# One block fewer in the expert pipeline of a transformer layer: 135 instead of 136

## The chip, the cores and the metric

The kernel runs on one core of a Trainium2 chip. The metric is the device time of one execution in microseconds (us). A core has five engines that run their own instruction streams and meet at semaphores: TensorE (PE, with its weight loads PEld), VectorE (DVE), ScalarE (ACT), GpSimd (POOL) and SyncE (SP), and 16 DMA engines that move data for the queues of SP, POOL and ACT.

## What is computed

The input is `x` of 4 batches x 2048 tokens x 256 values, all float32. One adaLN transformer layer is applied: attention with one head of 128, then a feed-forward part with one shared and eight routed experts, of which each token takes two. The second half, cut to its core:

```python
h = _layernorm(x) * (1 + cb) + sb
shared = (silu(h @ shared_gate.T) * (h @ shared_up.T)) @ shared_down.T
probs = sigmoid(h @ router_w.T + routing_bias)
scores, indices = top_k(probs, 2);  scores /= scores.sum(-1)
g, u = silu(h @ gate_w[e]), h @ up_w[e]          # each expert e, width 512
combined = sum over e of w[:, e] * ((g * u) @ down_w[e])
x = x + gb * (shared + combined)
```

The routed experts are computed by blocks. A block is 128 rows (tokens) that all go to one expert. There are 2 x 8192 = 16,384 rows to place, which is 128 full blocks, and each of the eight experts rounds its rows up to whole blocks.

## The kernel before

`attention_phase` does the attention and leaves the new `x` in device memory. `ffn_phase` does the rest as one pipeline of steps, each over one tile of 128 rows by 512 intermediate values:

- steps 0 to 39 (`ALL` = 32 + 8) run tiles through the shared expert. The first 32 also route two tiles each and scatter the normalised rows into `x_rows`, sorted by expert;
- steps 40 to 175 are the `NBLK` = 136 expert blocks. POOL loads a block's rows from `x_rows`, PE turns them and multiplies them with the weights of the block's expert, ACT scales the result, and POOL scatters it into `y_rows`;
- steps `L0` = 176 to 199 run the `LATE` = 24 remaining tiles through the shared expert. Meanwhile the finished rows are fetched in `CHUNKS` = 32 chunks of two tiles: SP reads a token's first expert result from `y_rows`, POOL adds the second by DMA, DVE multiplies by the gate (`gate_chunk`, L1573) and adds to the output tile (`output_chunk`, L1579), and SP stores.

Every step looks the same on PE, in this order: the down projection of the step before last (12 matmuls, L31 to L33), the turning of the last step's products (4, L796), the turning of the next step's rows (2, L788), and gate and up of this step (12, L806). ACT and DVE split each result into a high and a low part in between: `act_products_high` (L830) then `dve_products_low` (L843) for the products, `act_silu` (L834) then `dve_products` (L849).

Steps alternate between two halves of every buffer; the half is called `par`. In the expert stage `par` is the parity of the block number `j`. Of the late tiles before, the half is the parity of `i`, their number from 0.

The order is written out by hand for each engine. `steps(eng, step)` (L1009) emits the expert stage: steps 0 to 3 as straight code, then a hardware loop (`Fori`) with two steps per iteration, then the last steps as straight code, because those end the flow of loads and start the late tiles. The loop runs from block 4 to block 133, 65 iterations. In the list of a block's expert numbers, PE reads one packed word for each pair of blocks (`experts`, L1340), which also holds the experts of the pair before: `who[0]` and `who[1]` are the pair before, `who[2]` and `who[3]` this pair.

DVE has in the late tiles, beside its part of the step, one chunk in one step and two in the next, by the rule `2 * (chunk + 1) <= 3 * (i - 2)`. A step with two chunks is called a double step below. There are ten of them.

Of the kernel before, what the change touches and what calls it, by code (L numbers as in the profile page):

```python
# [890 lines left out]
def ffn_phase(nc, d, router_w, router_bias, out):  # L891
# [11 lines left out]
    T = P * NT  # L903
    STEPS = d.steps
    ALL = STEPS + d.extra
    NBLK = d.blocks
    L0 = ALL + NBLK
    LATE = NT - ALL
    GROUPS = len(d.groups)
# [9 lines left out]
    with ExitStack() as ctx:  # L919
# [50 lines left out]
        behind = h_rows[PLAN_GROUP % RING].rearrange("p s t h -> p (s t h)")[:, 0:NBLK * E].rearrange(  # L970
            "p (m e) -> p m e", e=E)
        over = behind[:, 0:d.most, :].rearrange("p m e -> p (m e)").rearrange("p (e m) -> p e m", e=E)
        moved_by = sb("moved_by", [P, NBLK], F32)
        expert_of = sb("expert_of", [1, NBLK + 2], F32)
        packed = sb("packed", [1, 3, NBLK // 2], F32)
        free_i = sb("free_i", [1, E], I32)

        w_loaded = [sem(f"s_w_loaded{i}") for i in range(2)]
# [32 lines left out]
        def steps(eng, step):  # L1011

            for j in range(4):
                step(j, j % 2)
            with eng.Fori(2, NBLK // 2 - 1) as i:
                step(2 * i, 0)
                step(2 * i + 1, 1)
            step(NBLK - 2, 0)
            step(NBLK - 1, 1)

        def both_halves(m, o):

# [26 lines left out]
        def _(sp):  # L1049
# [32 lines left out]
            for e in range(1, E):  # L1082
                if e >= 2:

                    end = sp.value_load(d.ends_i[0:1, e - 2:e - 1], min_val=1, max_val=NBLK)
# [8 lines left out]
                sp.dma_start(slots[:, k % SLOTS], y_v[0, :, C * k:C * k + C, :]).then_inc(y_in[k % SLOTS], 16)  # L1094

            sp.wait_ge(f.y_mm, L0)
            for s in y_sent:
                sp.wait_ge(s, 16 * (NBLK // 2))
            for k in range(SLOTS):
                load(k)  # L1100
            for k in range(CHUNKS):
# [9 lines left out]
        def _(pool):  # L1111
# [36 lines left out]
            load(0, 0)  # L1148
            load(1, 1)
            steps(pool, step)  # L1150
            scatter(NBLK - 2, 0)
            scatter(NBLK - 1, 1)
            for k in range(CHUNKS):
                pool.wait_ge(y_in[k % SLOTS], 16 * (k // SLOTS + 1))
                pool.dma_start(slots[:, k % SLOTS], y_v[1, :, C * k:C * k + C, :], accum_op=ALU.add
# [3 lines left out]
        def _(act):  # L1159
# [67 lines left out]

            def step(j, par):
                if isinstance(j, int) and j >= NBLK - 2:
                    normalise_single(d.extra + par)  # L1230
                if inside(j - 2, NBLK):
                    output(j - 2, par)
                f.act_products_high(act, j + (ALL - 1), 1 - par)
                if inside(j + 1, NBLK):
                    f.act_rows_high(act, j + (ALL + 1), 1 - par)
                else:
                    single_high(d.extra)
                f.act_silu(act, j + ALL, par)

            steps(act, step)  # L1240
            for i in range(LATE):
                s = d.extra + i
                if i + 2 < LATE:
                    normalise_single(s + 2)
                if i < 2:
                    output(NBLK - 2 + i, i)
                f.act_products_high(act, L0 + i - 1, (i - 1) % 2)
                if i + 1 < LATE:
                    single_high(s + 1)
                f.act_silu(act, L0 + i, i % 2)  # L1250
            f.act_products_high(act, L0 + LATE - 1, (LATE - 1) % 2)

        @block.tensor
        def _(pe):
# [115 lines left out]
            down(last - 1, 0, shared_weights)  # L1370
            f.pe_turn_products(pe, last, 1)
            down(last, 1, shared_weights)

        @block.vector
        def _(dve):
# [139 lines left out]
            def plan_experts():  # L1515
                op(dve.memset(starts[:, 0:1], 0.0))
                op(dve.tensor_copy(starts[:, 1:E + 1], ends[:]))
                op(dve.scalar_tensor_tensor(out=moved[:], in0=starts[:], scalar=-float(P), in1=d.first_row[:, 0:E + 1],
                                            op0=ALU.mult, op1=ALU.add))
                op(dve.tensor_tensor(jump[:], moved[:, 1:E + 1], moved[:, 0:E], ALU.subtract))  # L1520
                op(dve.tensor_tensor(behind, c.numbers[:].unsqueeze(2).to_broadcast([P, NBLK, E]),
                                     ends[:].unsqueeze(1).to_broadcast([P, NBLK, E]), ALU.is_ge))
# [3 lines left out]
                digit = [by_pair[:, 0:NBLK // 2, 0], by_pair[:, 0:NBLK // 2, 1],  # L1526
                         by_pair[:, 1:NBLK // 2 + 1, 0], by_pair[:, 1:NBLK // 2 + 1, 1]]
# [5 lines left out]
                op(dve.tensor_copy(d.table[:, 1, 0:NBLK // 2], packed[:, 0]))  # L1533

            def plan_rows():
                op(dve.tensor_tensor(behind, behind, jump[:].unsqueeze(1).to_broadcast([P, NBLK, E]), ALU.mult))
                op(dve.tensor_reduce(moved_by[:], behind, AX_X, ALU.add))
                op(dve.tensor_tensor(d.block_rows[:], c.own_rows[:], moved_by[:], ALU.add))
                op(dve.tensor_copy(d.table[:, 0], d.block_rows[0:1]))
# [98 lines left out]
                    rides(j + 1, 1 - par)  # L1638

            steps(dve, step)  # L1640
            tell(NBLK - 1, 1)
            chunk = 0
            for i in range(LATE):
                m = L0 + i
                if i >= 2:
                    gated(m - 2)
                f.dve_products_low(dve, m - 1, (i - 1) % 2)
# [4 lines left out]
                f.dve_products(dve, m, i % 2)  # L1652
# [4 lines left out]
            f.dve_products_low(dve, L0 + LATE - 1, (LATE - 1) % 2)  # L1657
            gate_chunk(chunk)
            for m in (L0 + LATE - 2, L0 + LATE - 1):
                gated(m)  # L1660
# [169 lines left out]
```

## Time and profile before

| | |
|---|---|
| median of 3 runs | 1679.46 us (1678.69 to 1680.17) |
| the profiled execution's own time | 1678.08 us |
| its span, first to last instruction | 1676.5 us |
| mean granted TensorE clock | 0.993 |
| PE busy | 1636.4 us, 98% |
| DVE busy | 1084.4 us, 65% |
| ACT busy | 816.7 us, 49% |
| POOL busy | 618.3 us, 37% |

Busy time is the time in which an engine had at least one instruction in work; matmuls overlap, so the busy time of PE isn't the sum of its instructions. The stretches, in us from the span's start: attention up to about 640, the first shared tiles up to about 890, the expert blocks from there to about 1551, the late tiles to the end. The chain of waits is the profile's own reading of which work ended last, followed back from the last instruction: a piece stands there with its start and with the time that it holds the chain.

### The profile page before, as it was taken

The page shows a single profiled execution, that of the slowest core. Times are in us where ns is not written, and L with a number is a line of the kernel's source. Part 1 is how long each engine was busy: PE and PEld are TensorE (multiplying, and loading weights), DVE is VectorE, ACT ScalarE, POOL GpSimd, SP SyncE. Part 2 cuts the span into 40 slices and gives each one's busy share as a digit, 9 for nine tenths or more (in the row PEclk, how much of TensorE's full clock was granted, in tenths as well). Part 3 has the DMA queues.
Part 4 walks back from the last instruction along what each step waited for, and adds up shares of the span by engine and source line. Part 5 has one row for each costly group of instructions (what it writes and reads, how often), then busy time and mean ns, then how long its engine had stood idle before and what let it go on. Part 6 is the DMA issues. An engine that isn't in the chain of part 4 may idle for free.

```text
span 1676.5 us, 35991 instructions
## 1 busy us (share of the span) xinstructions
PE 1636.4 (98%) x10888; PEld 1475.1 (88%) x10889; DVE 1084.4 (65%) x2655; ACT 816.7 (49%) x1599; POOL 618.3 (37%) x687
## 2 busy tenths in 40 slices
PE   8899999999999988999989999999999999999998
PEld 7799999999999977888878888888888888888887
DVE  7777787778778766888774444444444444444688
ACT  6565656565655544555453333333333333334554
POOL 3444346434523000465662333333333333333331
PEclk9999999999999998999999999999999999999999
DMA  3234433443344606122233223133223332111896
GB/s 120 89 114 139 132 127 114 139 132 126 107 146 145 233 33 214 53 94 83 91 117 101 70 89 97 54 118 114 83 79 116 116 111 75 50 57 51 191 257 162
DMA packets 110598, 190.10 MB, mean 113 GB/s; under 512 B 15140, under 2 KB 75172, under 8 KB 110252
## 3 DMA queue, kind: packets, MB, share of 16 engines
q1 hardware_dynamic: 81484, 125.40, 23.4%
q0 software_dynamic: 27904, 61.39, 12.7%
q10 hardware_dynamic: 1120, 2.10, 0.3%
q8 instruction: 58, 0.95, 0.3%
q14 instruction: 32, 0.26, 0.1%
HBM read 106.73 MB, written 82.10 MB: 113 GB/s over the span
## 4 chain that ended last, share of the span: by engine, by line
PE 55%; DVE 6%; ACT 1%; issue 1%; DMA 0%; DVEq 0%
PE f_bank L806 32%; PE f_bank L31 5%; PE f_bank L33 5%; PE f_bank L32 5%; PE f_bank L796 5%; PE f_bank L788 3%; DVE f_prod L849 1%; DVE f_aT_lo L843 1%; DVE scaled L1379 0%; ACT w_all L1170 0%; DVE f_xT_lo L838 0%; DVE Z L1417 0%; DVE w_all L1411 0%; DVE more_rows L1387 0%; DMA rw_raw<-in_router_w 0%
## 5 line engine op out<-in xcount | busy, mean ns | idle before, releaser
L806 PE MATMUL f_bank<-w_all,f_xT_hi 128*128 x1088 | 353.4, 406 | 0.7 <-issue 0.6
L849 DVE TENSOR_TENSOR f_prod<-f_silu_g,f_bank 128x512 f32<-128x512 f32 x200 | 137.5, 687 | 210.0 <-PE f_bank L806 209.1
L843 DVE TENSOR_TENSOR f_aT_lo<-f_bank,f_aT_hi 128x512 fp32r<-128x512 f32 x200 | 137.9, 689 | 160.2 <-ACT f_aT_hi L830 160.1
L806 PEld LDWEIGHTS f_bank<-w_all,f_xT_hi 128*128 128x128 f32 x1088 | 194.4, 188 | 38.7 <-issue 1.8
L1225 ACT ACTIVATE more_rows<-f_bank,score 128x256 f32<-128x256 f32 x136 | 64.6, 475 | 330.7 <-PE f_bank L33 328.9
L1131 POOL DMA_DIRECT2D more_rows<-x_rows x136 | 75.1, 552 | 382.7 <-PE f_bank L788 372.2
L806 PE MATMUL f_bank<-w_all,f_xT_lo 128*128 x544 | 214.5, 394 | 0.0
L830 ACT ACTIVATE f_aT_hi<-f_bank 128x512 fp32r<-128x512 f32 x200 | 118.5, 592 | 139.6 <-PE f_bank L796 139.6
L806 PE MATMUL f_bank<-w_shared,f_xT_hi 128*128 128x512 f32 x512 | 185.2, 438 | 0.0
L834 ACT ACTIVATE f_silu_g<-f_bank 128x512 f32<-128x512 f32 x200 | 119.2, 596 | 115.0 <-PE f_bank L806 115.0
L658 DVE TENSOR_REDUCE bmax<-s_pair 128x1 f32<-128x512 f32 (+1 forms) x192 | 166.3, 867 | 12.0 <-PE s_pair L33 8.6
L396 ACT ACTIVATE pT_hi<-t_pair 128x512 fp32r<-128x512 f32 (+1 forms) x192 | 135.8, 747 | 77.8 <-PE t_pair L520 76.2
L677 DVE TENSOR_TENSOR pT_lo<-t_pair,pT_hi 128x512 fp32r<-128x512 f32 (+1 forms) x192 | 160.2, 862 | 16.1 <-ACT pT_hi L396 14.1
L389 ACT ACTIVATE prob<-s_pair,negmax 128x1024 f32<-128x1024 f32 x128 | 141.6, 1114 | 57.6 <-DVE negmax L670 51.7
L1137 POOL DMA_INDIRECT y_rows<-more_rows,goes_to x136 | 137.0, 1007 | 86.3 <-issue 64.8
L33 PE MATMUL f_bank<-w_all,f_aT_lo 128*128 x544 | 152.3, 280 | 0.0
L32 PE MATMUL f_bank<-w_all,f_aT_hi 128*128 x544 | 151.7, 279 | 0.0
L31 PE MATMUL f_bank<-w_all,f_aT_hi 128*128 x544 | 151.7, 279 | 0.0
L31 PE MATMUL o_bank<-pT_hi,v_hi 128*128 128x256 f32 x512 | 145.9, 285 | 0.0
L33 PE MATMUL o_bank<-pT_hi,v_lo 128*128 128x256 f32 x512 | 144.0, 281 | 0.0
L32 PE MATMUL o_bank<-pT_lo,v_hi 128*128 128x256 f32 x512 | 143.7, 281 | 0.0
L520 PE MATMUL t_pair<-ident,prob 128*128 128x128 f32 x1024 | 132.9, 273 | 4.7 <-ACT prob L389 4.7
(253 smaller groups left out, 4158.0 us busy)
## 6 DMA issues: line engine op xcount, KB each, us to landing
w_all<-w_parts SPq DMA_DIRECT2D x84, 256.0 KB, 2.7
more_rows<-x_rows POOLq DMA_DIRECT2D x136, 130.0 KB, 2.4
w_parts<-piece_hi SPq DMA_DIRECT2D x27, 512.0 KB, 2.6
w_parts<-piece_raw SPq DMA_DIRECT2D x27, 512.0 KB, 3.6
XS<-in_x SPq DMA_DIRECT2D x32, 256.0 KB, 3.0
XR<-in_x SPq DMA_DIRECT2D x32, 256.0 KB, 2.8
x<-XR SPq DMA_DIRECT2D x32, 256.0 KB, 4.4
Z<-x SPq DMA_DIRECT2D x4, 2048.0 KB, 11.7
```

The source lines that it names most:

```text
L31: pe.matmul(out, l_hi, r_hi, start=first, stop=False)
L32: pe.matmul(out, l_hi, r_lo, start=False, stop=False)
L33: return pe.matmul(out, l_lo, r_hi, start=False, stop=last)
L389: act.activation(prob[:, c, PAIR * h:PAIR * h + PAIR], s_pair[h][:], ACT.Exp, bias=negmax[:, c:c + 1], accum_out=esum[:, G % 2, c, h:h + 1 ...
L396: act.activation(pT_hi[:, r:r + 4 * n, P * c:P * c + P], t_pair[:, 512 * i:512 * (i + n)].rearrange("p (k q) -> p k q", q=P), ACT.Copy).th ...
L520: mm = pe.transpose(t_pair[:, 512 * i + P * k:512 * i + P * k + P], prob[:, c, o:o + P], ident[:])
L658: dve.tensor_reduce(bmax[:, c, i:i + 1], ap, AX_X, ALU.max).then_inc(max_done, 1)
L677: dve.tensor_tensor(pT_lo[o], t_pair[:, 512 * i:512 * (i + n)].rearrange("p (k q) -> p k q", q=P), pT_hi[o].bitcast(F32), ALU.subtract).th ...
L806: mm = pe.matmul(out[:, 0:I], l, w, start=(c == 0 and k == 0), stop=(c == HC - 1 and k == 2))
L843: dve.tensor_tensor(flat(aT_lo, par), a_bank[:, 0:I], flat(aT_hi, par).bitcast(F32), ALU.subtract).then_inc(f.aT_lo_done, 1)
L849: dve.tensor_tensor(prod[:, par, :], silu_g[:, par, :], u_bank[:, 0:I], ALU.mult).then_inc(f.prod_done, 1)
L1137: pool.indirect_dma_start(d.y_rows, bass.IndirectOffsetOnAxis(ap=goes_to[:, par, :], axis=0), y[:, par, :], None).then_inc(y_sent[par], 16)
```

## The change

`NBLK` becomes one less than the count of blocks in the tables, 135. The tables that the plan fills on DVE keep their size (136, now called `B`). With 16,384 rows and at most 127 rows of rounding for each expert, the real blocks are at most floor((16,384 + 8 x 127) / 128) = 135, so block 135 holds only filler rows whatever the input.

`L0` becomes 175, an odd number. Everything that took the half of a late tile from `i` takes it from the step number. The loop in `steps` runs from block 4 to block 131, 64 iterations, and three steps (132, 133, 134) follow as straight code in place of two.

```diff
-    NBLK = d.blocks
+    B = d.blocks
+    NBLK = B - 1
...
             with eng.Fori(2, NBLK // 2 - 1) as i:
                 step(2 * i, 0)
                 step(2 * i + 1, 1)
-            step(NBLK - 2, 0)
-            step(NBLK - 1, 1)
+            for j in range(NBLK // 2 * 2 - 2, NBLK):
+                step(j, j % 2)
...
-            for s in y_sent:
-                sp.wait_ge(s, 16 * (NBLK // 2))
+            for par in range(2):
+                sp.wait_ge(y_sent[par], 16 * ((NBLK + 1 - par) // 2))
...
-            scatter(NBLK - 2, 0)
-            scatter(NBLK - 1, 1)
+            scatter(NBLK - 2, NBLK % 2)
+            scatter(NBLK - 1, (NBLK - 1) % 2)
...
-                    normalise_single(d.extra + par)
+                    normalise_single(d.extra + j - (NBLK - 2))
...
-                    output(NBLK - 2 + i, i)
-                f.act_products_high(act, L0 + i - 1, (i - 1) % 2)
+                    output(NBLK - 2 + i, (NBLK + i) % 2)
+                f.act_products_high(act, L0 + i - 1, (L0 + i - 1) % 2)
...
-                down(m - 2, i % 2, weights_of(who[2 + i]) if i < 2 else shared_weights)
-                f.pe_turn_products(pe, m - 1, (i - 1) % 2)
+                down(m - 2, m % 2, weights_of(who[1 + i]) if i < 2 else shared_weights)
+                f.pe_turn_products(pe, m - 1, (m - 1) % 2)
...
-                f.pe_gate_up(pe, m, i % 2, shared_weights)
+                f.pe_gate_up(pe, m, m % 2, shared_weights)
```

The same renaming of halves is made in the late part of DVE (`f.dve_products_low`, `f.dve_products`) and for the last two down projections. Lines below L905 stand one lower in the new file.

How the instructions move is seen best on ACT, behind the loop of the expert stage. Before, this is what follows the loop's branch: step 134, then step 135, which already normalises and turns the first late tiles (L1179 is `normalise_single`, L1193 and L1197 are `single_high`, L826 is the high part of a block's rows).

```order
L1015 COMPARE_AND_BRANCH
L1179 ACTIVATE more_rows<-Z,offset,rstd 128x256
L1225 ACTIVATE more_rows<-f_bank,score 128x256
L830 ACTIVATE f_aT_hi<-f_bank 128x512
L826 ACTIVATE f_xT_hi<-f_bank 128x256
L834 ACTIVATE f_silu_g<-f_bank 128x512
L1179 ACTIVATE more_rows<-Z,offset,rstd 128x256
L1225 ACTIVATE more_rows<-f_bank,score 128x256
L830 ACTIVATE f_aT_hi<-f_bank 128x512
L1193 ACTIVATE more_rows<-f_bank,mod_cols 128x128 x2
L1197 ACTIVATE f_xT_hi<-more_rows 128x256
L834 ACTIVATE f_silu_g<-f_bank 128x512
```

In the changed kernel, the same place of ACT:

```order
L1016 COMPARE_AND_BRANCH
L1226 ACTIVATE more_rows<-f_bank,score 128x256
L830 ACTIVATE f_aT_hi<-f_bank 128x512
L826 ACTIVATE f_xT_hi<-f_bank 128x256
L834 ACTIVATE f_silu_g<-f_bank 128x512
L1180 ACTIVATE more_rows<-Z,offset,rstd 128x256
L1226 ACTIVATE more_rows<-f_bank,score 128x256
L830 ACTIVATE f_aT_hi<-f_bank 128x512
L826 ACTIVATE f_xT_hi<-f_bank 128x256
L834 ACTIVATE f_silu_g<-f_bank 128x512
L1180 ACTIVATE more_rows<-Z,offset,rstd 128x256
L1226 ACTIVATE more_rows<-f_bank,score 128x256
```

A plain block step (four instructions, step 132) stands between the branch and what was there; the rest follows unchanged, one line number on.

On POOL, what follows the loop before (L1137 is the scatter of a block's result, L1155 the adding of a chunk by DMA):

```order
L1015 COMPARE_AND_BRANCH
L1137 DMA y_rows<-more_rows,goes_to 16512x256 x4
L1155 DMA w_all<-y_rows 128x2x256 x32
L919 UNCONDITIONAL_BRANCH
```

and in the changed kernel:

```order
L1016 COMPARE_AND_BRANCH
L1131 TENSOR_LOAD table
L1131 ISA x2
L1132 ISA
L1132 DMA more_rows<-x_rows 128x260
L1138 DMA y_rows<-more_rows,goes_to 16512x256 x5
L1156 DMA w_all<-y_rows 128x2x256 x32
L920 UNCONDITIONAL_BRANCH
```

The load of the last block and one scatter have come out of the loop into straight code. With one loop iteration less (two loads, two scatters), POOL does one load and one scatter less in all. PE has 49 more rows of this kind in its straight code and DVE 7; each runs one step less.

## Rows read from the trace of the kernel before

**Rows 1.** The page, part 1: busy time, share of the span and instructions.
```profile
PE 1636.4 (98%) x10888; PEld 1475.1 (88%) x10889; DVE 1084.4 (65%) x2655; ACT 816.7 (49%) x1599; POOL 618.3 (37%) x687
```
**Rows 2.** Busy time by stretch: expert blocks, then late tiles; columns as labelled.
```profile
core 0: us, PE busy (x) PEld busy (x) DVE busy (x) ACT busy (x) POOL busy (x), PEclk, DMA share, GB/s
1200.00:1450.00 250.00, 249.81 (x1546) 221.49 (x1545) 115.28 (x362) 93.80 (x205) 79.62 (x102) 1.00 0.30 92
...
1560.00:1676.50 116.50, 110.81 (x686) 97.56 (x684) 94.97 (x179) 57.34 (x127) 38.50 (x32) 1.00 0.93 217
```
**Rows 3.** Chain of waits, one block step and the two after: start, us, what.
```profile
1541.89 0.44 PE f_bank L796 x4
1542.33 0.22 PE f_bank L788 x2
1542.55 2.79 PE f_bank L806 x12
1545.34 0.12 PE f_bank L31
...
1546.75 0.44 PE f_bank L796 x4
...
1551.61 0.44 PE f_bank L796 x4
```
**Rows 4.** Line L1225, ACT, one instruction per block: durations, first and last start.
```profile
L1225 ACT ACTIVATE more_rows<-f_bank,score x136: 474/475/477, 898.2 to 1556.6; 128x256 f32<-128x256 f32 x136
```
**Rows 5.** Chain of waits inside one of the longer block steps.
```profile
1186.71 0.19 issue
1186.90 3.06 PE f_bank L806 x12
```
**Rows 6.** ACT timeline, L1225: two loop iterations, then two straight steps apart.
```profile
1488.70 0.47 ACT L1225 ACTIVATE more_rows<-f_bank,score 128x256 f32<-128x256 f32 x1 [2.41 <-PE f_bank L33]
...
1498.42 0.47 ACT L1225 ACTIVATE more_rows<-f_bank,score 128x256 f32<-128x256 f32 x1 [2.41 <-PE f_bank L33]
...
1542.04 0.47 ACT L1225 ACTIVATE more_rows<-f_bank,score 128x256 f32<-128x256 f32 x1 [1.83 <-PE f_bank L33]
...
1551.75 0.47 ACT L1225 ACTIVATE more_rows<-f_bank,score 128x256 f32<-128x256 f32 x1 [1.78 <-DVE goes_to L1564]
```
**Rows 7.** DVE timeline of the late tiles: start, us, what [idle before <-releaser].
```profile
1571.44 0.69 DVE L1573 TENSOR_TENSOR w_all<-w_all,mod_rows 128x512 f32<-128x512 f32 x1 [0.98 <-DMA w_all<-y_rows]
...
1627.05 0.68 DVE L843 TENSOR_TENSOR f_aT_lo<-f_bank,f_aT_hi 128x512 fp32r<-128x512 f32 x1
...
1635.05 0.69 DVE L1573 TENSOR_TENSOR w_all<-w_all,mod_rows 128x512 f32<-128x512 f32 x1
1636.20 0.69 DVE L1579 TENSOR_TENSOR Z<-Z,w_all 128x512 f32<-128x512 f32 x1 [0.46 <-DVE w_all L1573]
...
1670.47 0.68 DVE L1573 TENSOR_TENSOR w_all<-w_all,mod_rows 128x512 f32<-128x512 f32 x1
```
**Rows 8.** PE timeline, late tiles: a down projection's start, then two turnings.
```profile
1627.92 0.28 PE L31 MATMUL f_bank<-w_shared,f_aT_hi 128*128 128x256 f32 x1
...
1634.21 0.60 PE L796 MATMUL f_bank<-ident,f_prod 128*128 128x128 f32 x4
...
1639.40 0.60 PE L796 MATMUL f_bank<-ident,f_prod 128*128 128x128 f32 x4
```
**Rows 9.** DMA queues, 895 to 1550 us: packets, MB, share of 16 engines.
```profile
q8 instruction: 3, 0.05, 0.0%
```
**Rows 10.** The same for 1550 to 1676.5 us; last the median us to landing.
```profile
q8 instruction: 6, 0.10, 0.3%
...
w_all<-y_rows POOLq DMA_DIRECT2D x32, 256.0 KB, 6.7
```
**Rows 11.** POOL timeline of the late tiles: first eight chunks, last chunk.
```profile
1563.37 9.91 POOL L1155 DMA_DIRECT2D w_all<-y_rows  x8 [4.54 <-DMA w_all<-y_rows]
...
1654.19 1.19 POOL L1155 DMA_DIRECT2D w_all<-y_rows  x1 [1.96 <-DMA w_all<-y_rows]
```

More of the change, by code:

```diff
@@ L969, in ffn_phase @@
         PLAN_GROUP = GROUPS - 3
-        behind = h_rows[PLAN_GROUP % RING].rearrange("p s t h -> p (s t h)")[:, 0:NBLK * E].rearrange(
+        behind = h_rows[PLAN_GROUP % RING].rearrange("p s t h -> p (s t h)")[:, 0:B * E].rearrange(
             "p (m e) -> p m e", e=E)
         over = behind[:, 0:d.most, :].rearrange("p m e -> p (m e)").rearrange("p (e m) -> p e m", e=E)
-        moved_by = sb("moved_by", [P, NBLK], F32)
-        expert_of = sb("expert_of", [1, NBLK + 2], F32)
-        packed = sb("packed", [1, 3, NBLK // 2], F32)
+        moved_by = sb("moved_by", [P, B], F32)
+        expert_of = sb("expert_of", [1, B + 2], F32)
+        packed = sb("packed", [1, 3, B // 2], F32)
         free_i = sb("free_i", [1, E], I32)
@@ L1083, in _ @@
                 if e >= 2:
-                    end = sp.value_load(d.ends_i[0:1, e - 2:e - 1], min_val=1, max_val=NBLK)
+                    end = sp.value_load(d.ends_i[0:1, e - 2:e - 1], min_val=0, max_val=NBLK)
                     hold(sp, d, f.y_mm, end + ALL)
@@ L1245, in _ @@
                 if i < 2:
-                    output(NBLK - 2 + i, i)
-                f.act_products_high(act, L0 + i - 1, (i - 1) % 2)
+                    output(NBLK - 2 + i, (NBLK + i) % 2)
+                f.act_products_high(act, L0 + i - 1, (L0 + i - 1) % 2)
                 if i + 1 < LATE:
                     single_high(s + 1)
-                f.act_silu(act, L0 + i, i % 2)
-            f.act_products_high(act, L0 + LATE - 1, (LATE - 1) % 2)
+                f.act_silu(act, L0 + i, (L0 + i) % 2)
+            f.act_products_high(act, L0 + LATE - 1, (L0 + LATE - 1) % 2)
         @block.tensor
@@ L1363, in _ @@
                 m = L0 + i
-                down(m - 2, i % 2, weights_of(who[2 + i]) if i < 2 else shared_weights)
-                f.pe_turn_products(pe, m - 1, (i - 1) % 2)
+                down(m - 2, m % 2, weights_of(who[1 + i]) if i < 2 else shared_weights)
+                f.pe_turn_products(pe, m - 1, (m - 1) % 2)
                 if i + 1 < LATE:
                     turn(m + 1)
-                f.pe_gate_up(pe, m, i % 2, shared_weights)
+                f.pe_gate_up(pe, m, m % 2, shared_weights)
             last = L0 + LATE - 1
-            down(last - 1, 0, shared_weights)
-            f.pe_turn_products(pe, last, 1)
-            down(last, 1, shared_weights)
+            down(last - 1, (last - 1) % 2, shared_weights)
+            f.pe_turn_products(pe, last, last % 2)
+            down(last, last % 2, shared_weights)
         @block.vector
@@ L1520, in plan_experts @@
                 op(dve.tensor_tensor(jump[:], moved[:, 1:E + 1], moved[:, 0:E], ALU.subtract))
-                op(dve.tensor_tensor(behind, c.numbers[:].unsqueeze(2).to_broadcast([P, NBLK, E]),
-                                     ends[:].unsqueeze(1).to_broadcast([P, NBLK, E]), ALU.is_ge))
+                op(dve.tensor_tensor(behind, c.numbers[:].unsqueeze(2).to_broadcast([P, B, E]),
+                                     ends[:].unsqueeze(1).to_broadcast([P, B, E]), ALU.is_ge))
                 op(dve.memset(expert_of[:, 0:2], 0.0))
@@ L1525, in plan_experts @@
                 by_pair = expert_of[:].rearrange("o (i two) -> o i two", two=2)
-                digit = [by_pair[:, 0:NBLK // 2, 0], by_pair[:, 0:NBLK // 2, 1],
-                         by_pair[:, 1:NBLK // 2 + 1, 0], by_pair[:, 1:NBLK // 2 + 1, 1]]
+                digit = [by_pair[:, 0:B // 2, 0], by_pair[:, 0:B // 2, 1],
+                         by_pair[:, 1:B // 2 + 1, 0], by_pair[:, 1:B // 2 + 1, 1]]
                 so_far = digit[3]
@@ L1532, in plan_experts @@
                     so_far = packed[:, k]
-                op(dve.tensor_copy(d.table[:, 1, 0:NBLK // 2], packed[:, 0]))
+                op(dve.tensor_copy(d.table[:, 1, 0:B // 2], packed[:, 0]))
             def plan_rows():
-                op(dve.tensor_tensor(behind, behind, jump[:].unsqueeze(1).to_broadcast([P, NBLK, E]), ALU.mult))
+                op(dve.tensor_tensor(behind, behind, jump[:].unsqueeze(1).to_broadcast([P, B, E]), ALU.mult))
                 op(dve.tensor_reduce(moved_by[:], behind, AX_X, ALU.add))
@@ L1640, in _ @@
             steps(dve, step)
-            tell(NBLK - 1, 1)
+            tell(NBLK - 1, (NBLK - 1) % 2)
             chunk = 0
@@ L1646, in _ @@
                     gated(m - 2)
-                f.dve_products_low(dve, m - 1, (i - 1) % 2)
+                f.dve_products_low(dve, m - 1, (m - 1) % 2)
                 if i + 1 < LATE:
@@ L1651, in _ @@
                     shared_out(m - 2)
-                f.dve_products(dve, m, i % 2)
+                f.dve_products(dve, m, m % 2)
                 while chunk < CHUNKS - 1 and 2 * (chunk + 1) <= 3 * (i - 2):
@@ L1656, in _ @@
                     chunk += 1
-            f.dve_products_low(dve, L0 + LATE - 1, (LATE - 1) % 2)
+            f.dve_products_low(dve, L0 + LATE - 1, (L0 + LATE - 1) % 2)
             gate_chunk(chunk)
```

## The prediction

> **What bounds the kernel.** I read the page first, then the stretches, then the chain of waits around the place of the change, then the timelines of the engines that feed PE there. The page gives PE 1636.4 us of busy time in a span of 1676.5 us [rows 1]; the next engine, DVE, has 65%. An average over the whole kernel doesn't say what one step is worth, so the stretches come next. In 250 us of the expert stage PE is busy for 249.81 us, at full granted clock, while DVE works 115 us and the DMA engines are busy 30% of the time [rows 2]. Nothing but PE holds this stage. In the late tiles PE is busy 110.81 of 116.50 us, DVE 94.97, and the DMA engines 93% [rows 2]: PE still leads there, but with neighbours that are nearly full.
>
> The chain of waits shows the same from inside: around the last blocks it consists of PE pieces alone, turning of products 0.44 us, turning of rows 0.22, gate and up 2.79, and the twelve matmuls of the down projection from 1545.34 to 1546.75, which is 1.41 [rows 3]. Their sum is 0.44 + 0.22 + 2.79 + 1.41 = 4.86 us, and from one turning to the next the chain shows exactly that: 1541.89, 1546.75, 1551.61 [rows 3]. The last two of these distances are around blocks 134 and 135, the very blocks at the edge of the change, and one of them is pure filler.
>
> **The change, part by part.**
>
> *One step less.* All engines issue one block step less. On PE, which has no idle time in it, this is worth the whole period: 4.86 us by the rows beside the place [rows 3]. Over the whole stage, ACT's output instruction runs 136 times with first start at 898.2 and last at 1556.6 [rows 4], a mean of 658.4 / 135 = 4.88 us. The surplus over 135 x 4.86 is 658.4 - 656.1 = 2.3 us for the whole stage. It sits in a few longer steps; inside one of them the chain has 0.19 us of issue time and 3.06 us in place of 2.79 for gate and up [rows 5], 0.46 us in all. The step that goes is a regular one. I take -4.86 us. The ends for this term are -4.86 and, if one longer step goes as well, -5.32.
>
> *A loop iteration for a straight step.* The change removes one iteration, which is two steps, and adds one straight step. In the loop two outputs of ACT that are one iteration apart lie 1498.42 - 1488.70 = 9.72 us apart; in the straight code behind it two steps take 1551.75 - 1542.04 = 9.71 us [rows 6]. So a looped step and a straight step cost the same within 0.01 us, and the branch back costs nothing on the path. The difference is 2 x 4.86 - 4.86 = 4.86 again, and this term adds nothing: 0.
>
> The instruction fetches can be seen in the trace as packets of the queues called instruction: three on the busier of them in 655 us of the expert stage against six in the 126 us behind it [rows 9, 10]. The loop is not fetched again at each turn. The Trainium skill, "Runtime: NRT & Kernel Launch", section "Instruction fetch mechanics", says that a taken branch whose target isn't in the two pages at hand forces a fetch and a stall, and that kernels therefore prefer unrolled code. By that rule each removed iteration would also give back a stall, and the change would bring more than a step; the trace shows neither fetches nor a longer period in this loop, so the sum stays as it is.
>
> *The other half of the buffers.* The late tiles start in half 1 in place of half 0. The two halves of a buffer are alike in shape, and the late tiles use both in turn, before and after. In the chain a step of half 0 (1541.89 to 1546.75) and one of half 1 (to 1551.61) take the same 4.86 us [rows 3]. Only the two ends change: the first tile in half 1, the last in half 0. The cost is 0; the bound from both sides is the last digit of these rows, 0.01 us a step, over 24 steps 0.24 us.
>
> *POOL and SP.* The load of the last block now stands in straight code behind a read of the table. It is one of 135 and its queue has slack: PE leads, and POOL's instructions wait for PE. SP waits for both semaphores of the scatters with 68 and 67 in place of 68 and 68; both waits end when the last scatter has landed, which is as far behind the last block as before. The transfers of the chunks hang on the end of the blocks, not on a clock time, so they move forward with it. Cost 0; if the cover failed, the first chunk would come later, which is taken up below.
>
> *The plan's tables* keep their size; 0.
>
> *Code that shifts.* Behind the loop PE's straight code begins with one more step, so the places where the instruction stream crosses from one fetched piece to the next move against the work. One hole is visible: DVE ends L1573 at 1635.74 and begins the dependent L1579 at 1636.20 [rows 7], 0.46 us idle, which the row puts down to nothing but DVE itself. That was in a double step, and those have next to no slack: in the one before it, DVE's low part ends at 1627.05 + 0.68 = 1627.73 and PE's down projection starts at 1627.92 [rows 7, 8], 0.19 us later. So PE lost time: from one turning to the next it took 1639.40 - 1634.21 = 5.19 us [rows 8], 0.33 more than 4.86. If the hole falls into a single step, where DVE has one chunk less and so 2 x 0.69 = 1.4 us more slack, these 0.33 us come back; if three more such holes meet double steps, the late part loses 1 us. That gives -0.33 to +1.0. I take 0, since a hole of this kind is as likely to stay as to go, and its place can't be read off.
>
> **The sum.** -4.86 + 0 + 0 + 0 + 0 = -4.86 us. Against the profiled execution's own 1678.08 us (its span 1676.5 and 1.6 us around it) that is 1673.2 us. That execution was 1.38 us faster than the median of the runs, 1679.46. The forecast for the median is 1679.46 - 4.86 = 1674.6 us, 0.29% less.
>
> **Rivals.**
>
> *A. The gain is partly given back in the late tiles.* The mechanism is the one of the holes and of the first chunks. DVE waited 0.98 us for the first chunk's transfer [rows 7], and POOL needs 9.91 us to issue the first eight of them [rows 11], with the double step right behind. In the ten double steps every delay of DVE beyond 0.2 us is one of PE. Should the first three double steps lose 0.5 us each and two more holes 0.33 us each, the sum is 1.5 + 0.66 = 2.2 us back, which gives 1676.8 us. For it: the DMA engines are 93% busy and the slack is 0.2 us. Against it: before, only one of ten double steps lost anything, and nothing in the order of the chunks changes.
>
> *B. More than a step.* One of the long steps goes, and the hole at 1635 misses the double step: -4.86 - 0.33 - 0.46 = -5.65, that is 1673.8 us. For it: such steps come and go without a cause that the program shows.
>
> *C. Slower: the stream of chunks becomes the bound of the late tiles.* If the transfers came so late that DVE waited for each chunk, each wait would sit in front of DVE's low part in the same engine, and PE's down projection waits for that. The point from which this decides is the distance at the end: POOL issues the last addition at 1654.19 [rows 11] and DVE uses that chunk at 1670.47 [rows 7]. With 1.19 us of issue and 6.7 us to land [rows 10], the stream is 8 us ahead. It would have to fall 8 us back for the first loss, and 8 + 4.86 + 3.4 = 16 us for a kernel that is slower by over 0.2%, in 116 us. A case that lands at 20 us behind gives 1679.5 + 20 - 8 - 4.9 = 1686.6 us. For it only the DMA share of 93%; against it, the transfers are the same in number, size and order, and start at the same distance from the last block.
>
> *D. The change saves nothing,* because what goes was idle time. For that PE would have to wait in the last blocks. It does not [rows 3]. It would give 1679.5 us.
>
> **Chances.** The forecast 84%, with its own range of 1673.6 to 1675.9 us; A 7%; B 5%; C 2%; D 2%. Two measurements of this kernel can tell about 0.2% from no change, which is 3.4 us, so the line is at 1676.1 us. The forecast lies 1.5 us below it. The three runs of before spread by 1.5 us in all, so a small part of the forecast's mass falls above the line; together with A and D this makes "within 0.2%" 8%. Slower is C and a rest, 2%. Faster is 90%. The range for 8 times in 10 reaches from B's side, 1673.2, to half way into A, 1676.2.
>
> **What would show it.** In the new profile the output instruction of ACT (now L1226) runs 135 times; the distance from its first to its last start is 134 x 4.88 = 653.5 us, 4.9 less. The turnings of PE behind the loop stay 4.86 us apart for steps 132, 133 and 134. PE's busy time falls by 4.9 us with its share unchanged, matmuls by 30. From the last output of ACT (1556.6 before) to the end of the span it takes 119.9 us as before, within 0.5. The forecast is wrong if that last stretch is longer by over 1 us (A, C), if a gap stands between the loop's end and step 132, or if the expert stage has no less time for one block fewer (D).

## The result and the profile after

The changed kernel takes 1674.06 us (median of 7 runs, 1672.21 to 1674.83) against 1679.72 us (7 runs, 1678.69 to 1680.62), a ratio of 0.9968 with a 95% interval from 0.9958 to 0.9978. That is 5.7 us less, and by the ratio's interval between 3.7 and 7.1 us. Forecast were 4.86 us less, with a range that ended at 1673.2 and 1676.2 us.

Part 1 of the page after, which answers to [rows 1]: PE has 30 matmuls less, as a step has, and its share of the span is the same.

```profile
PE 1634.3 (98%) x10858; PEld 1474.4 (88%) x10859; DVE 1081.4 (65%) x2648; ACT 814.0 (49%) x1595; POOL 616.3 (37%) x685
```

The stretches of expert blocks and of late tiles, in the columns of [rows 2] (us, busy time by engine, granted clock, DMA share, GB/s): PE still fills every microsecond of the first and has the same neighbours in the second.

```profile
1340.00:1545.00 205.00, 205.00 (x1266) 181.93 (x1265) 94.33 (x295) 79.09 (x174) 65.07 (x84) 1.00 0.22 69
1555.00:1673.00 118.00, 112.35 (x694) 99.07 (x692) 95.39 (x181) 58.63 (x131) 39.03 (x33) 1.00 0.92 216
```

The chain of waits behind the loop, which answers to [rows 3]: the turnings in the steps of blocks 131 to 134 and of the first three late tiles start 4.85 to 4.88 us apart, with the same pieces in them. There is no gap where the loop ends, and none where the late tiles begin in half 1.

```profile
1528.92 0.44 PE f_bank L796 x4
...
1533.78 0.44 PE f_bank L796 x4
...
1538.63 0.44 PE f_bank L796 x4
1539.07 0.22 PE f_bank L788 x2
1539.29 2.80 PE f_bank L806 x12
1543.49 0.44 PE f_bank L796 x4
...
1548.34 0.44 PE f_bank L796 x4
...
1553.21 0.44 PE f_bank L796 x4
...
1558.09 0.44 PE f_bank L796 x4
```

ACT's output instruction, which answers to [rows 4] (durations, first and last start):

```profile
L1226 ACT ACTIVATE more_rows<-f_bank,score x135: 473/473/477, 900.5 to 1553.4; 128x256 f32<-128x256 f32 x135
```

This line divides the span into three parts that are read with little noise: up to the first output, from the first to the last, and the rest. Before: 898.2, 658.4 and 119.9 us. After: 900.5, 652.9 and 119.6. So the expert stage gave 5.5 us and the rest 0.3. The first part took 2.3 us more, in attention and routing, which the change doesn't touch: that is why the two spans, 1676.5 and 1673.0, differ by only 3.5 us while the medians differ by 5.7.

In the late tiles, the DVE timeline after has the same hole of 0.47 us between L1574 and L1580, but in another place than in [rows 7]: behind the first chunk, 104 us before the end, and not in a double step 40 us before it.

```profile
1567.90 0.69 DVE L1574 TENSOR_TENSOR w_all<-w_all,mod_rows 128x512 f32<-128x512 f32 x1 [0.70 <-DMA w_all<-y_rows]
1569.07 0.69 DVE L1580 TENSOR_TENSOR Z<-Z,w_all 128x512 f32<-128x512 f32 x1 [0.47 <-DVE w_all L1574]
```

The steps around the place of the old hole, on the timeline of ACT (L830, one per step), are 4.86 and 4.88 us long; the answering one in [rows 8] had 5.19.

```profile
1631.63 0.60 ACT L830 ACTIVATE f_aT_hi<-f_bank 128x512 fp32r<-128x512 f32 x1 [2.16 <-PE f_bank L796]
1636.49 0.60 ACT L830 ACTIVATE f_aT_hi<-f_bank 128x512 fp32r<-128x512 f32 x1 [2.14 <-PE f_bank L796]
1641.37 0.60 ACT L830 ACTIVATE f_aT_hi<-f_bank 128x512 fp32r<-128x512 f32 x1 [2.16 <-PE f_bank L796]
```

The stream of chunks ends as far ahead as in [rows 11]: POOL issues the last addition at 1648.47, and DVE begins with that chunk at 1666.94, 18.5 us later (16.3 before).

```profile
1648.47 1.19 POOL L1156 DMA_DIRECT2D w_all<-y_rows  x1 [0.50 <-issue]
...
1666.94 0.68 DVE L1574 TENSOR_TENSOR w_all<-w_all,mod_rows 128x512 f32<-128x512 f32 x1
```

### The profile page after: what moved, and what is told of

The parts are those of the page before. It is cut to its first block, busy times and chain, and to the rows that moved or that the text cites. A ratio compares the mean times of both kernels' runs of the same rounds, so it can differ in the third digit from the quotient of the medians.

```text
span 1673.0 us, 35843 instructions
## 1 busy us (share of the span) xinstructions
PE 1634.3 (98%) x10858; PEld 1474.4 (88%) x10859; DVE 1081.4 (65%) x2648; ACT 814.0 (49%) x1595; POOL 616.3 (37%) x685
## 4 chain that ended last, share of the span: by engine, by line
PE 56%; DVE 5%; ACT 1%; issue 0%; DMA 0%; DVEq 0%
PE f_bank L806 32%; PE f_bank L31 5%; PE f_bank L33 5%; PE f_bank L32 5%; PE f_bank L796 5%; PE f_bank L788 3%; DVE f_prod L849 1%; DVE f_aT_lo L843 1%; DVE scaled L1380 0%; ACT w_all L1171 0%; DVE f_xT_lo L838 0%; DVE w_all L1412 0%; DVE Z L1418 0%; DVE more_rows L1388 0%; DMA rw_raw<-in_router_w 0%
## 5 line engine op out<-in xcount | busy, mean ns | idle before, releaser
L830 ACT ACTIVATE f_aT_hi<-f_bank 128x512 fp32r<-128x512 f32 x199 | 117.7, 591 | 140.5 <-PE f_bank L796 140.5
L677 DVE TENSOR_TENSOR pT_lo<-t_pair,pT_hi 128x512 fp32r<-128x512 f32 (+1 forms) x192 | 160.1, 861 | 16.3 <-ACT pT_hi L396 14.2
L31 PE MATMUL f_bank<-w_all,f_aT_hi 128*128 x540 | 150.6, 279 | 0.0
L31 PE MATMUL o_bank<-pT_hi,v_hi 128*128 128x256 f32 x512 | 145.9, 285 | 0.0
```

Source lines behind the costliest of these rows:

```text
L31: pe.matmul(out, l_hi, r_hi, start=first, stop=False)
L677: dve.tensor_tensor(pT_lo[o], t_pair[:, 512 * i:512 * (i + n)].rearrange("p (k q) -> p k q", q=P), pT_hi[o].bitcast(F32), ALU.subtract).th ...
```

## Experiments

The experiments ran in three sets, each with the kernel before timed beside them. In the first two sets (135 again, 132, 137 and 140 blocks; then the extra instructions, the even spread and the unrolled kernel) the stretch between attention and the first expert block was longer: the first output of ACT came at 983 to 1006 us in place of 898 to 901. The kernel before was slower there too, 1767.08 and 1784.18 us, so times are compared within a set only. The parts from the first output on are compared across all traces; kernels of one count scatter there by about 1 us.

### Other counts of blocks

The change once more, and three other counts of blocks:

```diff
-    NBLK = B - 1
+    NBLK = B - 4          # 132 blocks; B - 2 for 134, B for 140
-    d.blocks = TOP * T // P + E
+    d.blocks = TOP * T // P + E + 2      # with B - 1: 137; + 4 and B: 140
```

> The changed kernel once more, beside the kernel before and with three other counts of blocks on the same chip. Theory 1 (a step is worth PE's period and nothing else changes): 4.9 us less than before, 1674.8 us against 1679.7. Theory 2 (the odd count brings something of its own, since the first timing gave 5.7 us and not 4.9): again 5.5 us or more.

> 132 blocks, all of which hold real rows for these inputs; an even count, so late tiles begin in half 0 as before. Theory 1: 4 x 4.86 = 19.4 us less than the 136 blocks of before, 1660.3 us. Theory 2 (half 1 at the start of the late tiles is worth -0.8 us): the even counts 132, 136, 140 lie on one line of 4.86 us per block and the odd ones 135 and 137 both lie 0.8 us under it. Rival 3 (steps without the cover of others cost more or less near the end): the slope changes from 136 to 132.

> 137 blocks (tables of 138), odd, five of them filler. Theory 1: 4.86 us more than before, 1684.6 us. Theory 2: 4.86 - 0.8 = 4.1 us more, 1683.8 us.

> 140 blocks (tables of 140), even, eight of them filler. Theory 1: 4 x 4.86 = 19.4 us more than before, 1699.1 us. The slope between 132 and 140 gives the price of a block with an error of a tenth of a microsecond: theory 1 says 4.86, the mean with the longer steps 4.88; a filler block that cost less than a real one would show as less than 4.86 here.

> 134 blocks (real ones: 132), even; tables of 136. Theory 1: 2 x 4.86 = 9.7 us less than before; from first to last output 647.9 us. Theory 2 (half 1 as the late tiles' first is worth -0.8 us against half 0): 8.9 us less than before and only 4.1 less than 135.

> The kernel before, unchanged, with a trace on the chip of this set, to be read by stages against the traces of 135 blocks there. Theory 1 (a step is worth PE's period): from the first to the last output of ACT 5.0 us more than the 652.7 to 653.7 us of the 135-block kernels, 658 to 659 us; the part after the last output 119.6 to 119.9 us. Theory 2 (the odd count brings something of its own in the late tiles): the part after the last output is longer than 119.7 by 0.5 us or more.

| blocks | median us (runs) | before in the set | ratio (interval) | first to last output | a step | rest |
|---|---|---|---|---|---|---|
| 136, the first trace | 1679.72 (7) | | | 658.4 | 4.877 | 119.9 |
| 136 again | 1678.89 (11) | 1680.10 (21) | 0.9995 (0.9986 to 1.0004) | 658.6 | 4.879 | 119.9 |
| 135, the first trace | 1674.06 (7) | 1679.72 | 0.9968 (0.9958 to 0.9978) | 652.9 | 4.872 | 119.6 |
| 135 again | 1761.63 (12) | 1767.08 (18) | 0.9974 (0.9960 to 0.9987) | 653.7 | 4.878 | 119.6 |
| 134 | 1669.35 (5) | 1680.10 | 0.9938 (0.9924 to 0.9951) | 648.7 | 4.877 | 119.9 |
| 132 | 1745.25 (5) | 1767.08 | 0.9884 (0.9864 to 0.9905) | 638.8 | 4.876 | 120.7 |
| 137 | 1773.54 (6) | 1767.08 | 1.0043 (1.0029 to 1.0057) | 665.4 | 4.893 | 120.3 |
| 140 | 1787.17 (5) | 1767.08 | 1.0133 (1.0112 to 1.0154) | 680.2 | 4.894 | 120.5 |

The lines of the second trace of 136 blocks and of 134 blocks, from which the last columns are read as above:

```profile
L1225 ACT ACTIVATE more_rows<-f_bank,score x136: 474/475/478, 898.2 to 1556.8; 128x256 f32<-128x256 f32 x136
```

```profile
L1226 ACT ACTIVATE more_rows<-f_bank,score x134: 473/473/477, 899.2 to 1547.9; 128x256 f32<-128x256 f32 x134
```

From 136 to 134, both even, the median falls by 10.75 us and by 9.5 against the same program timed as a candidate, around twice 4.86. The 135 blocks stand in the middle of the two. In all kernels of this table whose tables have 136 entries, a step is 4.87 to 4.88 us, odd or even, so the filler step was worth what every step is worth, and theory 1 stands. Theory 2 is wrong as I had put it: nothing of 0.8 us hangs on odd or even. A small difference sits in the rest: 119.9 with 136 and 134 blocks, 119.6 with 135. It goes with the number of straight steps behind the loop (two or three) and not with odd or even, as the next section shows with 136 blocks. The counts 134 and 132 are for measuring only: they compute the layer for these inputs, but not for any input.

The whole times by themselves are too rough for the question. 135 again was 5.4 us below before, between the 4.9 of theory 1 and the 5.5 of theory 2. 132 blocks gave 21.8 us where 19.4 were forecast, and 137 blocks cost 6.5 us where 4.9 or 4.1 were. By stages, 132 blocks take 19.5 us less from first to last output than the average of three traces of 136, which is 4 x 4.88, and 134 take 9.6 less, which is 2 x 4.8.

The forecasts for 137 and 140 were missed in one point. Their steps take 4.893 and 4.894 us, and two steps of the loop take 9.75 us on the timeline of ACT where the others take 9.71. These are the two kernels with longer tables (138 and 140 entries), so that the buffers behind may lie elsewhere; whether that is the cause isn't shown. PE has no idle time there either (100.00 of 100 us, from 1500 to 1600 with 137 blocks), and I didn't find what costs the 0.3 to 0.4%. For the price of a block they are of no use.

The rest of 132 blocks, 120.7, has one step of 5.52 us in which DVE waited 1.99 us for the transfer of the first chunk (0.98 in the kernel before), and the double step behind it took 4.99 us. Together that is the 0.8 us above 119.9. This is the mechanism of rival A, in one of the twelve traces of experiments.

```profile
1644.10 0.69 DVE L1574 TENSOR_TENSOR w_all<-w_all,mod_rows 128x512 f32<-128x512 f32 x1 [1.99 <-DMA w_all<-y_rows]
```

### The hole on DVE and the length of the straight code

The loop of the kernel before ends one iteration earlier; four steps follow in straight code:

```diff
-            with eng.Fori(2, NBLK // 2 - 1) as i:
+            with eng.Fori(2, NBLK // 2 - 2) as i:
...
-            step(NBLK - 2, 0)
-            step(NBLK - 1, 1)
+            for j in range(NBLK - 4, NBLK):
+                step(j, j % 2)
```

> 136 blocks as before; the loop ends one iteration earlier and four steps stand behind it as straight code. So the straight code is longer by two steps and its fetches shift, and no work goes. Theory 1: the same time as before within 0.5 us; first to last output 658.4, the rest 119.6 to 119.9. Rival (the code's place behind the loop decides over holes of DVE or PE in the late tiles): the part after the last output differs from 119.9 by the 0.33 us of a hole, or more.

1679.12 us (11 runs), ratio 0.9989 (0.9980 to 0.9999); the unchanged kernel, in the same set as a candidate, had 0.9995, so the whole times don't tell them apart. The parts: 657.9 and 119.7, and there is no hole of this kind in its late tiles. The difference to 119.9 is smaller than the 0.33 us of the hole, since its first double step took 4.99 us. Seen over all traces the hole is not an accident. With two straight steps behind the loop it comes at the same distance from the end each time: 40.3 to 40.5 us before the end of the span, in both traces of 136 blocks and with 132, 134 and 140. The rows are of the second trace of 136 and of the one of 134:

```profile
1636.38 0.69 DVE L1579 TENSOR_TENSOR Z<-Z,w_all 128x512 f32<-128x512 f32 x1 [0.46 <-DVE w_all L1573]
```

```profile
1627.46 0.69 DVE L1580 TENSOR_TENSOR Z<-Z,w_all 128x512 f32<-128x512 f32 x1 [0.46 <-DVE w_all L1574]
```

With three straight steps it comes behind the first chunk, in each of seven traces, and there it costs nothing, since that step has slack. With four, and in the unrolled kernel, none is seen; one that falls where DVE waits anyhow would not be. So the place of the code in DVE's stream decides over it. That it has to do with the fetch of instructions fits this but isn't shown. No packet of the instruction queues lies within 1 us of a hole, but in all twelve traces that have one, a packet of queue 14 starts 2.1 to 3.8 us behind its end, while that queue has only three others in the late tiles. In the kernel before, whose hole ends at 1636.20, it is the first of these rows (1638 to 1639 us), in the changed one, 1569.07, the second (1572 to 1573):

```profile
q14 instruction: 1, 0.01, 1.9%
```

```profile
q14 instruction: 1, 0.01, 2.0%
```

The 0.46 us of idle time aren't the delay. Without a hole the dependent L1579 starts 0.79 us after L1573, as in the pair of instructions just before; with it the two are 1.15 us apart, 0.36 more.

```profile
1633.65 0.68 DVE L1573 TENSOR_TENSOR w_all<-w_all,mod_rows 128x512 f32<-128x512 f32 x1
1634.44 0.69 DVE L1579 TENSOR_TENSOR Z<-Z,w_all 128x512 f32<-128x512 f32 x1
```

### Slack of DVE in the late tiles

One more DVE instruction of 128x512 in each of the ten double steps; its result is not used:

```diff
+                if i >= 4 and i % 2 == 0:
+                    dve.tensor_tensor(scaled[:, 0, :, :], rows[:, 0:2, 0:H], rows[:, 0:2, 0:H], ALU.mult)
```

> 135 blocks; DVE has one more instruction of 128x512 in each double step of the late tiles (its result is not used), ten in all. Theory 1 (DVE has 0.19 us of slack in a double step and everything beyond it is PE's delay): an instruction takes 0.61 us start to start, so 10 x (0.61 - 0.19) = 4.2 us slower than the changed kernel, 1678.7. Rival (the late tiles have more float than the rows show, PE takes up the delay in the single steps between): less than 1 us slower.

1784.56 us against 1784.18 of before in the set (35 runs; one of them took 5666.65 us, which doesn't move the median), ratio 1.0008 (0.9996 to 1.0020). The changed kernel isn't in this set, so the cost is read by stages. First to last output takes 652.7 us as in the other traces of 135 blocks, the rest 125.4 in place of 119.6: 5.8 us more, where 4.2 were expected. Every double step has 5.44 us for 4.87. One of them, first on the timeline of DVE, then on that of PE with three turnings, of which the last two enclose it:

```profile
1730.50 0.69 DVE L1659 TENSOR_TENSOR scaled<-mod_rows 128x512 f32<-128x512 f32 x1
1731.11 0.42 DVE L1412 TENSOR_TENSOR more_rows<-f_bank,mod_rows 128x256 f32<-128x256 f32 x1
1731.44 0.68 DVE L843 TENSOR_TENSOR f_aT_lo<-f_bank,f_aT_hi 128x512 fp32r<-128x512 f32 x1
```

```profile
1732.18 0.39 PE L31 MATMUL f_bank<-w_shared,f_aT_hi 128*128 128x256 f32 x1 [0.31 <-DVE f_aT_lo L843]
1732.64 0.28 PE L31 MATMUL f_bank<-w_shared,f_aT_hi 128*128 128x256 f32 x1
...
1723.38 0.60 PE L796 MATMUL f_bank<-ident,f_prod 128*128 128x128 f32 x4
1728.26 0.60 PE L796 MATMUL f_bank<-ident,f_prod 128*128 128x128 f32 x4
1733.70 0.60 PE L796 MATMUL f_bank<-ident,f_prod 128*128 128x128 f32 x4
```

DVE's low part ends at 1731.44 + 0.68 = 1732.12, and PE starts 0.06 us later although it is waiting; this lag is the same in all ten double steps. So of the 0.19 us that I had called slack only 0.13 are. And the waiting costs a little by itself: from the first to the second L31 it is 0.46 us, again in all ten, where in the undisturbed step before it is 1727.20 - 1726.83 = 0.37 on the same timeline. 0.61 - 0.13 + 0.09 = 0.57, ten times 5.7 us. The same sum fits the hole: 0.36 - 0.13 + 0.09 = 0.32, and the step had 0.33 more. The rival is refuted: PE takes nothing up in the single steps.

The same ten instructions, with the chunks spread as three DVE instructions in every late step:

```diff
-                while chunk < CHUNKS - 1 and 2 * (chunk + 1) <= 3 * (i - 2):
-                    gate_chunk(chunk)
-                    output_chunk(chunk)
-                    chunk += 1
+                while chunk < CHUNKS - 1 and done < 3 * (i - 2) - 1:
+                    if done % 2 == 0:
+                        gate_chunk(chunk)
+                    else:
+                        output_chunk(chunk)
+                        chunk += 1
+                    done += 1
```

> 135 blocks; the chunks' instructions on DVE are spread as three in every late step in place of two and four in turn, beginning with two at i = 3. Theory 1: each late step then has 0.9 us of slack, a hole of 0.47 us of DVE no longer reaches PE; since only one hole in some runs cost 0.33 us, the time is that of the changed kernel within 0.4 us, 1674.0 to 1674.5. Rival (double steps lose more than the trace shows): 1 us or more faster.

> The even spread of the chunks with the same ten extra instructions of DVE as double_step_load. Theory 1: three chunk instructions of 0.7 us and the extra 0.61 fit into what the double step had, 0.28 us of slack are left, so it costs nothing: the time of even_chunks within 0.5 us. Rival (the extra work costs through something else than the place of DVE's low part, such as DVE's total): 4 us slower, as double_step_load.

Alone the even spread has 1780.24 us, ratio 0.9972 (0.9960 to 0.9985) to before, and a rest of 119.7. With the ten instructions it has 1777.01 us, ratio 0.9966 (0.9955 to 0.9977), and a rest of 119.7 too: the 5.8 us are gone. In the even spread DVE is done well ahead of PE, here at 1743.55 + 0.68 = 1744.23 for a down projection that starts at 1745.21, on the timelines of DVE and PE:

```profile
1743.55 0.68 DVE L843 TENSOR_TENSOR f_aT_lo<-f_bank,f_aT_hi 128x512 fp32r<-128x512 f32 x1
```

```profile
1745.21 0.28 PE L31 MATMUL f_bank<-w_shared,f_aT_hi 128*128 128x256 f32 x1
```

By the rest, both expectations of theory 1 held. The whole times don't show it as closely: with the ten instructions the median is 3.2 us lower than without, while 0.5 us had been allowed for, and in the two traces the stages up to the first output differ by 3.7 us (1002.6 and 1006.3), which neither edit touches. The even spread doesn't beat the changed kernel by anything that can be measured; its worth is that the late tiles no longer depend on where a hole falls. Of all kernels that compute the layer for any input, 135 blocks with either spread are the fastest, and these two can't be told apart.

### Straight code in place of the loop

```diff
-            with eng.Fori(2, NBLK // 2 - 1) as i:
-                step(2 * i, 0)
-                step(2 * i + 1, 1)
-            for j in range(NBLK // 2 * 2 - 2, NBLK):
+            for j in range(4, NBLK):
                 step(j, j % 2)
```

> 135 blocks, the 64 loop iterations (blocks 4 to 131) written out as straight code. Theory 1 (the branch costs nothing, a looped and a straight step take 4.86 us): the same time as the changed kernel within 1 us, about 1674.5, with some 25 more fetches of instructions on PE in the expert stage. Rival (each taken branch costs a fetch or a stall, 0.05 us or more): 3 us or more faster. Rival (straight code has to be fetched and PE waits for it): slower, each fetch at 0.3 to 0.5 us would be 8 to 12 us.

1781.36 us against 1784.18, ratio 0.9982 (0.9970 to 0.9994); the changed kernel was at 0.9974 in the set before. From first to last output it takes 654.4 us, and five traces of 135 blocks with the loop take 652.7 to 653.7. The DMA queues of the expert stage carry 46 and 28 instruction packets, where the loop has 3 and 2 (I had expected some 25 more on PE):

```profile
q8 instruction: 46, 0.75, 0.5%
q14 instruction: 28, 0.23, 0.1%
```

Neither rival holds. This difference by itself is the fetches less the branches and can't be split. The period splits it: in the unrolled kernel two steps of straight code take 9.71 us, as on these rows, and two steps of a loop iteration take 9.71 too. So 64 taken branches are worth nothing that shows, and 69 more fetches cost 0.7 to 1.7 us at most.

```profile
1414.44 0.47 ACT L1223 ACTIVATE more_rows<-f_bank,score 128x256 f32<-128x256 f32 x1 [2.31 <-PE f_bank L33]
...
1424.15 0.47 ACT L1223 ACTIVATE more_rows<-f_bank,score 128x256 f32<-128x256 f32 x1 [2.31 <-PE f_bank L33]
```

On the rule of the Trainium skill, "Runtime: NRT & Kernel Launch", section "Instruction fetch mechanics": its condition, a branch target outside the pages at hand, seems not to be met by this loop, since its code isn't fetched again (3 and 2 packets for 64 turns). The trace agrees with the rule so far, and no run here shows a loop that does meet the condition; unrolling, which kernels prefer for this reason by that section, brings nothing here.

### The longer block steps

For experts 2 to 7, each load of weights moves 8 of 512 columns. This kernel leaves the rest of the weights out and doesn't compute the layer; it is for timing only:

```diff
+                    n = PIECE if e == 1 else 8
-                    sp.dma_start(d.w_all[:, e % 2, 3 * W * part + o:3 * W * part + o + PIECE].bitcast(F32),
-                                 d.w_parts[e + 1, :, part, o:o + PIECE]).then_inc(d.w_ready, 16)
+                    sp.dma_start(d.w_all[:, e % 2, 3 * W * part + o:3 * W * part + o + n].bitcast(F32),
+                                 d.w_parts[e + 1, :, part, o:o + n]).then_inc(d.w_ready, 16)
```

> 135 blocks; for experts 2 to 7 each of the twelve loads of weights moves only 8 of 512 columns (the rest keeps what was there), with the same number of transfers and semaphores. In all traces so far the block steps longer than 4.97 us lie where weights are being loaded, one or two for each expert. Theory 1 (the longer steps come from the traffic of the weights): they go for experts 2 to 7, the mean of a block step falls from 4.872 to 4.860, 1.5 us less in the expert stage than the 652.9 us of the changed kernel. Rival (they come from the issue of loads or from the change of the weights' half on PE): they stay, 652.5 to 653.5 us.

1672.36 us (4 runs) against 1680.10, ratio 0.9955 (0.9940 to 0.9970). First to last output, by its line:

```profile
L1227 ACT ACTIVATE more_rows<-f_bank,score x135: 474/475/477, 899.2 to 1550.8; 128x256 f32<-128x256 f32 x135
```

That is 651.6 us, 4.863 a step. Three steps are longer than 4.97 us, two of them while expert 1 is loaded in full; the changed kernel has seven, the kernel before seven in this stage, its second trace nine. The count alone would be weak, since it scatters (the kernel with ten extra instructions has four). But in all thirteen traces with full loads at least two steps behind the first 260 us of the stage take more than 5.1 us, and in this one none takes more than 4.97. So the longer steps come with the traffic of the weights, as far as one trace without it can tell, and full loads cost 1.1 to 2.1 us in this stage (652.7 to 653.7 us in the five traces with them). How a transfer delays PE isn't shown by this, since the rows put it down to no one.

## Why the prediction was right

**One step less, -4.86.** Right, by its mechanism and its size. The period of PE in the chain held for the place that changed, and 134 blocks take 9.6 us less than 136 in this stage, for two steps.

**A loop iteration for a straight step, 0.** Right; the unrolled kernel has the same 9.71 us for two steps without a branch. I had written that each removed iteration would give back a stall by the rule on branches that I cited, and left out that this needs a branch target outside the pages at hand, which seems not to be the case in this loop; the sum didn't use it.

**The other half of the buffers, 0.** Right: 4.86 us from turning to turning through the new start of the late tiles, and no difference between odd and even that grows with their number.

**POOL, SP, tables, 0.** Right: the first chunk came after a wait of 0.70 us (0.98 before) and the last was no less ahead. That wait scatters, though, and where it was 1.99 us, with 132 blocks, it cost time.

**The longer steps.** I had said that the one that goes is a regular one and given -5.32 as the end if a longer one goes too. The first pair of traces has 5.5 us between them in this stage, since the longer steps summed to less by chance. Three traces of 136 blocks have 658.3 on average (658.4, 658.6, 657.9), five of 135 with the loop 653.0 (652.9, 653.7, 652.7, 652.9, 652.7): 5.3 us. Of this, 4.9 is the step; the 0.4 I put down to the scatter of the longer steps, which no run separates further. The longer end of this term was also too small: the step of [rows 5] has 0.32 us for the turning of rows in place of 0.22, which I didn't add, and is 5.42 us long, 0.56 more than a regular one and not 0.46. In the signs to look for, 134 x 4.88 is 653.9 and not 653.5, which goes with 4.877; measured were 652.9.

```profile
1185.95 0.44 PE f_bank L796 x4
1186.39 0.32 PE f_bank L788 x2
...
1191.37 0.44 PE f_bank L796 x4
```

**Code that shifts, -0.33 to +1.0, taken as 0.** This is the term that was mis-sized. It was -0.3: the hole left the double step. I had called its place impossible to read off; I can't read it off before a run either, but it is fixed by the code and not by chance, as it came back at 40.3 to 40.5 us before the end in each trace with two straight steps behind the loop. The slack of a double step, 0.19 in the prediction, is 0.13 and a wait costs 0.09 more.

Together the parts give 5.3 + 0.3 = 5.6 us, and the medians differ by 5.66. That they agree so closely is luck: the difference of the medians is known to 3.7 to 7.1 us only, and the stages before the first output, which no part covers, differ by 2.3 us between the first two traces. Rivals C and D are out: the stream of chunks kept its distance and the last blocks had no idle time in them. Rival A's mechanism exists, by the ten instructions and by the one late chunk at 132 blocks, but it didn't act in the changed kernel. Rival B was nearest in sum (1673.8 us). Its hole did leave the double step; its other half, a long step that goes, isn't shown, since both traces have seven of them and only their lengths differ.

## What to carry to other kernels

Where the chain of waits around the place of a change is one engine without a gap, a removed step is worth that engine's period, and the period is read from two neighbouring starts. Compare such changes by stages of the trace and not by the spans: here 2.3 us of scatter in an untouched stage hid two fifths of the effect. And slack between two engines counts only from where the signal has arrived; load the feeding engine on purpose, once with and once without an even spread of its work, to see how much there is.

## What the hardware showed that I had not expected

- A hole of 0.46 to 0.47 us on DVE between two dependent instructions, bound to the place in the code: it moved by 13 late steps when three straight steps stood in front of the late tiles in place of two.
- A matmul that had to wait for its input needed 0.46 us to the next of its kind instead of 0.37, and it started 0.06 us behind the end of the DVE instruction that it waited for.
- In the two kernels whose tables are 2 or 4 entries longer, every block step was 0.3 to 0.4% longer (9.75 us for two in place of 9.71), with no wait to show for it. Its cause stays open.
- In the second trace of 135 blocks, PE's granted clock from 640 to 985 us had a mean of 0.86 of full speed, so it was at the lower level, 1.2 GHz, for part of the time, and PE stood idle for 71 us. The trace before takes 258 us for this stretch, with a clock of 0.98. The kernel, attention and all later parts were the same, and all eight traces of the first two sets show it (0.84 to 0.88). What held the engines isn't told by the trace:

```profile
640.00:985.00 345.00, 273.86 (x1663) 237.89 (x1662) 200.46 (x565) 126.91 (x227) 129.99 (x132) 0.86 0.21 74
```
